# Three feature products of a step placed on two row halves of the TensorE array

## The chip, the cores and the metric

The kernel runs on one core of a Trainium2 chip. The time is that of the device for one execution of the whole program, in microseconds; where several executions were made, their median.

## What is computed

For each of 512 sequences, 128 steps follow one another. A step k takes 12 features of each sequence: four "flat" ones, of which the last (number 3) is replaced by the previous step's result from step 1 on, and eight "path" ones.

```python
def _tower(x, w_in, b_in, blocks):
    h = _leaky(x @ w_in + b_in)
    for w1, b1, w2, b2 in blocks:            # two blocks, 128x128 weights
        h = _leaky(_leaky(h @ w1 + b1) @ w2 + b2 + h)
    return h

def step(prev_delta, xk):
    fk, k = xk
    d = jnp.where(k == 0, fk[:, DELTA_IDX], prev_delta)
    fk = fk.at[:, DELTA_IDX].set(d)
    fe = _tower(fk[:, :N_FLAT], fw_in, fb_in, flat_blocks)
    pe = _tower(fk[:, N_FLAT:], pw_in, pb_in, path_blocks)
    h = _leaky(jnp.concatenate([fe, pe], axis=-1) @ cw1 + cb1)
    delta = jax.nn.sigmoid(h @ cw2 + cb2)[:, 0]
    return (delta, delta)
```

The output is delta for every step and sequence. Only the flat tower and the head depend on the step before; the path tower doesn't.

## The kernel before

Activations lie with the 128 hidden units on the partitions and the 512 sequences along the free axis. The flat tower and the head work in two groups of 256 columns (g = 0, 1), each with a PSUM bank of its own (`ps_flat`, `ps_head`), whose second half takes the feature product and the output product. The path tower works on all 512 columns at once (`ps_path1`, `ps_path2`), its hidden products in two halves of 256.

The hidden products (line 394), the head (L479 for the path's part, L484 for the flat part) and the output (L490) are fp32 and take two MATMUL instructions each, every one with a weight load (LDWEIGHTS). The feature products are different: `path_in` (L406) and `flat_x` (L450, once for each group) are fp32r, one MATMUL each. To keep the accuracy, features and weights are split into a high and a low part. The features' parts are written to memory in four chunks (`store_chunk`) and are loaded for each step in the order hi, hi, lo, lo into four 32-row quarters of a tile of 128 rows (`load_x`, L134); the weights `in_split` hold hi, lo, hi, lo of the weights in the same quarters. The rows that are not features are zero or, for the bias row, one. Each of the three feature products so runs over all 128 rows. `x_path` and `x_flat` are two tiles each, by the parity of the step.

The order of the work is written out by hand, once for each engine, in its `body(k, par)`. TensorE's (L493) is a software pipeline: body k holds the flat tower, head and output of step k, the last path products of step k + 1, the middle ones of k + 2, and the first ones of k + 3. `path_in(k + 3)` stands between the two halves of `path_2b(k + 1)`, with `combine_flat(k, 0)` behind it. `flat_x(k + 1, g = 0)` stands before `output(k, 0)` and `flat_x(k + 1, g = 1)` before `path_2a(k + 2)`.

Between the engines: ScalarE does the leaky activations of `p_in`, `p_mid`, `f_mid`, `f_res`, of the head (all L229) and the sigmoid `delta` (L277). VectorE adds bias and old value (`f_sum`, `p_sum`, L321), does the other leaky activations (L318), and `flat_delta` (L351): f_t = delta x its weight row + the product of flat_x, which needs the delta of its group and `s_f_x_mm` of its group. From f_t comes `f_in`, which the next step's `flat_1a` multiplies. SyncE issues the loads: `load_path` waits for path_in of two steps before, `load_flat` for both flat_x.

Of the kernel before, what the change touches and what calls it, by code (L numbers as in the profile page):

```python
# [9 lines left out]
GROUP_COLS = [(0, 256), (256, 512)]  # L10
GROUPS = len(GROUP_COLS)
HALF = BATCH // 2
QUAD = 32

CHUNK_STEPS = [8, 24, 48, 48]
CHUNKS = len(CHUNK_STEPS)
# [9 lines left out]
def build(nc, x, x_hi, x_lo, w, out):  # L26
# [4 lines left out]
    with ctx:  # L31
        def sb(name, shape, dt=fp32):
            return ctx.enter_context(nc.sbuf_tensor(name, shape, dt))
# [4 lines left out]
        def sem(name):  # L38
            return ctx.enter_context(nc.semaphore(name))
# [11 lines left out]
        cb2_col, cw2_rep = sb("cb2_col", [HID, 1]), sb("cw2_rep", [HID, HID])  # L51


        in_raw, in_split = sb("in_raw", [128, 2 * HID]), sb("in_split", [128, 2 * HID], fp32r)
        flat_in_w, path_in_w = in_split[:, 0:HID], in_split[:, HID:2 * HID]

        chunk_x = [sb(f"chunk_x{c}", [128, CHUNK_COLS[c]]) for c in range(CHUNKS)]
        chunk_hi = [sb(f"chunk_hi{c}", [128, CHUNK_COLS[c]], fp32r) for c in range(CHUNKS)]
        chunk_lo = [sb(f"chunk_lo{c}", [128, CHUNK_COLS[c]], fp32r) for c in range(CHUNKS)]

        x_flat = [sb(f"x_flat{p}", [128, BATCH], fp32r) for p in range(2)]
        x_path = [sb(f"x_path{p}", [128, BATCH], fp32r) for p in range(2)]

        p_in, p_mid1, p_mid2 = sb("p_in", [HID, BATCH]), sb("p_mid1", [HID, BATCH]), sb("p_mid2", [HID, BATCH])
        p_sum1, p_sum2 = sb("p_sum1", [HID, BATCH]), sb("p_sum2", [HID, BATCH])
# [18 lines left out]
        def second(b, g):  # L84
            lo, hi = GROUP_COLS[g]
            return b[g][:, hi - lo:2 * (hi - lo)]

        def cols(t, g):
            lo, hi = GROUP_COLS[g]
            return t[:, lo:hi]  # L90

        def half(t, h):
            return t[:, h * HALF:(h + 1) * HALF]

        s_in_zero, s_pads, s_in_loaded, s_in_hi, s_in_split = (
            sem(n) for n in ("s_in_zero", "s_pads", "s_in_loaded", "s_in_hi", "s_in_split"))
        s_w_loaded, s_columns, s_cw2, s_delta0 = (sem(n) for n in ("s_w_loaded", "s_columns", "s_cw2", "s_delta0"))
        s_chunk_loaded, s_chunk_hi, s_chunk_split, s_chunk_stored = (
            [sem(f"{n}{c}") for c in range(CHUNKS)]
# [31 lines left out]

        @block.sync
        def _(sp):
            def load_x(tile, loaded, rows, k, par):  # L134
                for q, part in enumerate((x_hi, x_hi, x_lo, x_lo)):
                    sp.dma_start(tile[par][q * QUAD + rows.start:q * QUAD + rows.stop, :].bitcast(fp32),
                                 part[k, rows, :]).then_inc(loaded[par], 16)

            def load_path(k, par):
                if not exists(k):  # L140
                    return
                if exists(k - 2):
                    sp.wait_ge(s_p_in_mm, k - 1)
                load_x(x_path, s_x_path, slice(N_FLAT, FEATS), k, par)

            def load_flat(k, par):
                if not exists(k):
                    return
                if exists(k - 2):
                    for g in range(GROUPS):  # L150
                        sp.wait_ge(s_f_x_mm[g], k - 1)
                load_x(x_flat, s_x_flat, slice(0, DELTA), k, par)

            def store_delta(k, par):
                if not exists(k):
                    return
                for g in range(GROUPS):
                    sp.wait_ge(s_delta[g], k + 1)
                sp.dma_start(out[k:k + 1, :], delta[par][0:1, :]).then_inc(s_stored[par], 16)

            def load_chunk(c):
                sp.dma_start(chunk_x[c][:, :], chunk_rows(x, c)).then_inc(s_chunk_loaded[c], 16)

            def store_chunk(c):
                sp.wait_ge(s_chunk_split[c], 1)
                sp.dma_start(chunk_rows(x_hi, c),
                             chunk_hi[c][:, :].bitcast(fp32)).then_inc(s_chunk_stored[c], 16)
                sp.dma_start(chunk_rows(x_lo, c),
                             chunk_lo[c][:, :].bitcast(fp32)).then_inc(s_chunk_stored[c], 16)

            def body(k, par):
                load_path(k, par)
                load_flat(k - 2, par)
                store_delta(k - 5, 1 - par)

            load_chunk(0)
            sp.wait_ge(s_in_zero, 1)
            for q in range(4):
                sp.dma_start(in_raw[q * QUAD:q * QUAD + FEATS + 1, :], w["inputs"]).then_inc(s_in_loaded, 16)
            sp.dma_start(hidden_w[:, :], w["hidden"]).then_inc(s_w_loaded, 16)  # L180
            sp.dma_start(delta[1][:, :], x[0, DELTA:DELTA + 1, :].to_broadcast([HID, BATCH])).then_inc(s_delta0, 16)
            store_chunk(0)
            sp.wait_ge(s_pads, 2)
            sp.wait_ge(s_chunk_stored[0], 32)
            body(0, 0)
            body(1, 1)
            for c in range(1, CHUNKS):
                load_chunk(c)
            for k in range(2, 6):
                body(k, k % 2)  # L190
            for c in range(1, CHUNKS):
                store_chunk(c)
            for c in range(CHUNKS):
                sp.wait_ge(s_chunk_stored[c], 32)
                for k in range(max(6, CHUNK_FIRST[c]), CHUNK_FIRST[c] + CHUNK_STEPS[c]):
                    body(k, k % 2)
            for k in range(STEPS, STEPS + 5):
                body(k, k % 2)
            for p in range(2):
                sp.wait_ge(s_stored[p], 8 * STEPS)  # L200

        @block.gpsimd
        def _(pool):
            pool.memset(in_raw[:, :], 0.0).then_inc(s_in_zero, 1)
            for tile in x_flat + x_path:
                last = pool.memset(tile[:, :].bitcast(fp32), 0.0)
            last.then_inc(s_pads, 1)
            pool.wait_ge(s_pads, 1)
            for tile in x_flat + x_path:
                last = pool.memset(tile[0:2 * QUAD, :].bitcast(fp32), 1.0)  # L210
            last.then_inc(s_pads, 1)
            pool.wait_ge(s_pads, 2)
            for c in range(1, CHUNKS):
                pool.wait_ge(s_chunk_loaded[c], 16)
                pool.tensor_copy(chunk_hi[c][:, :], chunk_x[c][:, :]).then_inc(s_chunk_hi[c], 1)
                pool.wait_ge(s_chunk_hi[c], 1)
                pool.tensor_tensor(chunk_lo[c][:, :], chunk_x[c][:, :], chunk_hi[c][:, :].bitcast(fp32),
                                   ALU.subtract).then_inc(s_chunk_split[c], 1)
# [80 lines left out]
        def _(dve):  # L299
# [3 lines left out]
            dve.tensor_tensor(chunk_lo[0][:, :], chunk_x[0][:, :], chunk_hi[0][:, :].bitcast(fp32),  # L303
                              ALU.subtract).then_inc(s_chunk_split[0], 1)

            dve.wait_ge(s_in_loaded, 64)
            dve.tensor_copy(in_split[:, :], in_raw[:, :]).then_inc(s_in_hi, 1)
            dve.wait_ge(s_in_hi, 1)
            for q in (1, 3):
                rows = slice(q * QUAD, (q + 1) * QUAD)  # L310
                dve.tensor_tensor(in_split[rows, :], in_raw[rows, :], in_split[rows, :].bitcast(fp32),
                                  ALU.subtract).then_inc(s_in_split, 1)

            dve.wait_ge(s_columns, 32)
            dve.tensor_copy(cw2_rep[:, :], column["cw2"].to_broadcast([HID, HID])).then_inc(s_cw2, 1)
# [76 lines left out]
        def _(pe):  # L392
# [7 lines left out]
            def path_in(k, par):  # L400
                if exists(k):
                    pe.wait_ge(s_x_path[par], filled(k, par))

                    if exists(k - 1):
                        pe.wait_ge(s_p1b_t, k)
                    pe.matmul(ps_path1[:, :], path_in_w, x_path[par][:, :], start=True, stop=True)\  # L406
                      .then_inc(s_p_in_mm, 1)

            def path_1a(k, h):
# [34 lines left out]
            def flat_x(k, par, g):  # L444
                if exists(k):
                    pe.wait_ge(s_x_flat[par], filled(k, par))

                    if exists(k - 1):
                        pe.wait_ge(s_f2b_t[g], k)
                    pe.matmul(second(ps_flat, g), flat_in_w, cols(x_flat[par], g), start=True, stop=True)\  # L450
                      .then_inc(s_f_x_mm[g], 1)

            def flat_1a(k, g):
# [39 lines left out]
            def body(k, par):  # L493
                flat_1a(k, 0)
                path_2a(k + 1, 1 - par, 1)
                flat_1a(k, 1)
                flat_1b(k, 0)
                combine_path(k, par, 0)
                flat_1b(k, 1)
                path_1b(k + 2, 0)  # L500
                flat_2a(k, 0)
                path_1b(k + 2, 1)
                flat_2a(k, 1)
                flat_2b(k, 0)
                combine_path(k, par, 1)
                flat_2b(k, 1)
                path_2b(k + 1, 0)
                path_in(k + 3, 1 - par)
                combine_flat(k, 0)
                path_2b(k + 1, 1)  # L510
                combine_flat(k, 1)
                flat_x(k + 1, 1 - par, 0)
                output(k, 0)
                path_1a(k + 3, 0)
                output(k, 1)
                path_1a(k + 3, 1)
                flat_x(k + 1, 1 - par, 1)
                path_2a(k + 2, par, 0)

            pe.wait_ge(s_w_loaded, 16)  # L520
            pe.wait_ge(s_in_split, 2)
            pe.wait_ge(s_cw2, 1)
            bodies(pe, body)

# [32 lines left out]
```

## Time and profile before

| | |
|---|---|
| Median of 3 runs | 1321.8 us (1321.71 to 1322.02) |
| The profiled execution's own time | 1322.16 us |
| Its span, first to last instruction | 1320.4 us |
| TensorE busy | 1296.7 us (98%), 6016 MATMULs |
| TensorE weight loads busy | 1071.2 us (81%), 6016 loads |
| VectorE busy | 853.9 us (65%) |
| ScalarE busy | 828.5 us (63%) |
| Mean granted TensorE clock | 0.999 of full speed |

The span leaves out 1.8 us of the execution's time, before the first and behind the last instruction. "Busy" of TensorE counts a matmul from its recorded start to a modelled end; matmuls are pipelined, so a new one begins before the record of the one before has ended. A MATMUL and its weight load are on two rows, PE and PEld. SPq is the queue of SyncE, from which DMAs are issued.

### The profile page before, as it was taken

Reading aid. Unit: us, or ns where it says so; the run is one execution under the profiler, and the core shown is the slowest. Engines: PE = TensorE matmul, PEld = TensorE weight load, DVE = VectorE, ACT = ScalarE, POOL = GpSimd, SP = SyncE. Lnnn points to the kernel's source line nnn. Section 1 sums busy time; section 2 is a strip of 40 time slices with the busy share of each in tenths; the row PEclk is TensorE's granted clock in tenths of the full one; section 3 lists DMA queues with packets and bytes.
Section 4 is the critical chain, followed back from the end, with each engine's and each line's share of the span. In section 5 each row is a group of like instructions: output and inputs, shape, how many; then the busy total and the mean of one; then the engine's idle time right before and its main releaser. Section 6 shows DMA issues by size and latency. Waiting matters only on the chain.

```text
span 1320.4 us, 18500 instructions
## 1 busy us (share of the span) xinstructions
PE 1296.7 (98%) x6016; PEld 1071.2 (81%) x6016; DVE 853.9 (65%) x1670; ACT 828.5 (63%) x1793; POOL 22.6 (2%) x19
## 2 busy tenths in 40 slices
PE   4999999999999999999999999999999999999998
PEld 2888888888888888888888888888888888888885
DVE  3666666666666666666666666666666666666665
ACT  2566666666666666666666666666666666666665
POOL 6000000000000000000000000000000000000000
PEclk9999999999999999999999999999999999999999
DMA  4400000000000000000000000000000000000000
GB/s 149 188 10 9 11 10 10 11 10 10 9 11 10 10 11 10 10 10 11 10 10 11 10 10 10 11 10 10 11 10 9 10 11 10 9 11 10 9 8 1
DMA packets 14022, 23.41 MB, mean 18 GB/s; under 512 B 6324, under 2 KB 6760, under 8 KB 13160
## 3 DMA queue, kind: packets, MB, share of 16 engines
q1 hardware_dynamic: 13640, 22.23, 5.7%
q8 instruction: 50, 0.82, 0.3%
q14 instruction: 44, 0.36, 0.1%
q10 hardware_dynamic: 288, 0.01, 0.0%
HBM read 15.66 MB, written 6.55 MB: 17 GB/s over the span
## 4 chain that ended last, share of the span: by engine, by line
PE 97%; DVE 1%; DMA 1%; ACT 0%; issue 0%; SPq 0%; ACTq 0%
PE ps_flat L394 34%; PE ps_path L394 34%; PE ps_head L479 8%; PE ps_head L484 8%; PE ps_head L490 8%; PE ps_path L406 2%; PE ps_flat L450 2%; DVE f_in L318 0%; DMA x_lo<-chunk_lo 0%; DVE f_t L351 0%; DMA chunk_x<-x 0%; DVE f_sum L321 0%; DVE p_sum L321 0%; DMA x_path<-x_lo 0%; ACT delta L277 0%
## 5 line engine op out<-in xcount | busy, mean ns | idle before, releaser
L229 ACT ACTIVATE f_mid<-ps_flat,columns_sb 128x256 f32<-128x256 f32 x512 | 242.4, 474 | 153.5 <-PE ps_flat L394 153.5
L394 PE MATMUL ps_path<-p_mid,hidden_w 128*128 128x256 f32 x1024 | 306.1, 381 | 0.8 <-ACT p_mid L229 0.8
L394 PE MATMUL ps_flat<-f_mid,hidden_w 128*128 128x256 f32 x1024 | 305.3, 380 | 0.0
L229 ACT ACTIVATE head<-ps_head,columns_sb 128x256 f32<-128x256 f32 x256 | 121.3, 474 | 246.0 <-PE ps_head L484 246.0
L394 PEld LDWEIGHTS ps_path<-p_mid,hidden_w 128*128 128x128 f32 x1024 | 195.9, 191 | 28.3 <-ACT p_mid L229 1.5
L394 PEld LDWEIGHTS ps_flat<-f_mid,hidden_w 128*128 128x128 f32 x1024 | 175.2, 189 | 46.2
L321 DVE SCALAR_TENSOR_TENSOR f_sum<-ps_flat,columns_sb,f_in 128x256 f32<-128x256 f32 x256 | 123.9, 484 | 129.1 <-PE ps_flat L394 129.1
L351 DVE SCALAR_TENSOR_TENSOR f_t<-delta,columns_sb,ps_flat 128x256 f32<-128x256 f32 x256 | 123.0, 480 | 98.3 <-ACT delta L277 93.3
L229 ACT ACTIVATE p_mid<-ps_path,columns_sb 128x512 f32<-128x512 f32 x256 | 174.8, 683 | 5.5 <-PE ps_path L394 5.5
L321 DVE SCALAR_TENSOR_TENSOR p_sum<-ps_path,columns_sb,p_in 128x512 f32<-128x512 f32 x128 | 96.1, 751 | 121.3 <-PE ps_path L394 121.3
L394 PE MATMUL ps_flat<-f_in,hidden_w 128*128 128x256 f32 x512 | 162.1, 398 | 5.1 <-DVE f_in L318 5.1
L394 PE MATMUL ps_path<-p_in,hidden_w 128*128 128x256 f32 x512 | 154.1, 384 | 1.6 <-ACT p_in L229 1.4
L394 PE MATMUL ps_flat<-f_res,hidden_w 128*128 128x256 f32 x512 | 153.0, 381 | 0.7 <-ACT f_res L229 0.7
L394 PE MATMUL ps_path<-p_res,hidden_w 128*128 128x256 f32 x512 | 153.1, 381 | 0.2 <-ACT p_res L229 0.2
L479 PE MATMUL ps_head<-p_res,hidden_w 128*128 128x256 f32 x512 | 152.8, 380 | 0.0
L490 PE MATMUL ps_head<-head,cw_rep 128*128 128x256 f32 x512 | 152.6, 380 | 0.2
L484 PE MATMUL ps_head<-f_res,hidden_w 128*128 128x256 f32 x512 | 152.4, 379 | 0.3 <-DVE f_res L318 0.3
L321 DVE SCALAR_TENSOR_TENSOR p_sum<-ps_path,columns_sb,p_res 128x512 f32<-128x512 f32 x128 | 96.1, 751 | 74.8 <-PE ps_path L394 74.8
L229 ACT ACTIVATE f_res<-f_sum 128x256 f32<-128x256 f32 x256 | 106.7, 417 | 58.5 <-DVE f_sum L321 58.4
L321 DVE SCALAR_TENSOR_TENSOR f_sum<-ps_flat,columns_sb,f_res 128x256 f32<-128x256 f32 x256 | 123.8, 484 | 17.5 <-PE ps_flat L394 3.3
L277 ACT ACTIVATE delta<-ps_head,cb_col 128x256 f32<-128x256 f32 x256 | 120.0, 469 | 10.0 <-PE ps_head L490 0.6
L450 PE MATMUL ps_flat<-x_flat,in_split 128*128 128x256 f32 x256 | 120.0, 469 | 0.0
(32 smaller groups left out, 1266.6 us busy)
## 6 DMA issues: line engine op xcount, KB each, us to landing
x_path<-x_hi SPq DMA_DIRECT2D x256, 16.0 KB
x_path<-x_lo SPq DMA_DIRECT2D x256, 16.0 KB
x_flat<-x_hi SPq DMA_DIRECT2D x256, 6.0 KB
x_flat<-x_lo SPq DMA_DIRECT2D x256, 6.0 KB
chunk_x<-x SPq DMA_DIRECT2D x2, 1152.0 KB, 7.8
x_hi<-chunk_hi SPq DMA_DIRECT2D x2, 1152.0 KB, 9.3
x_lo<-chunk_lo SPq DMA_DIRECT2D x2, 1152.0 KB, 10.8
out<-delta SPq DMA_DIRECT2D x128, 2.0 KB
```

The lines of the kernel that those rows point to most:

```text
L229: return act.activation(dst, src, ACT.Prelu, bias=bias, alpha=NEG)
L277: act.activation(cols(delta[par], g), second(ps_head, g), ACT.Sigmoid, bias=cb2_col[:, :]).then_inc(s_delta[g], 1)
L321: return dve.scalar_tensor_tensor(dst, products, bias, old, ALU.add, ALU.add)
L351: dve.scalar_tensor_tensor(f_t[g][:, :], cols(delta[1 - par], g), column["delta_w"], second(ps_flat, g), ALU.mult, ALU.add).then_inc(s_f_i ...
L394: return pe.matmul(dst, weight[w_name], src, start=True, stop=True)
L406: pe.matmul(ps_path1[:, :], path_in_w, x_path[par][:, :], start=True, stop=True)\
L450: pe.matmul(second(ps_flat, g), flat_in_w, cols(x_flat[par], g), start=True, stop=True)\
L479: pe.matmul(layer(ps_head, g), weight["cw1_path"], cols(p_res2[par], g), start=True, stop=False)
L484: pe.matmul(layer(ps_head, g), weight["cw1_flat"], f_res2[g][:, :], start=False, stop=True)\
L490: pe.matmul(second(ps_head, g), cw2_rep[:, :], head[g][:, :], start=True, stop=True)\
```

## The change

The two x tiles of a parity become one tile `x_both` of 128 rows: the path features (4 x 8 rows, the rest ones) in rows 0 to 63, the flat features (4 x 3 rows, the rest ones) in rows 64 to 127. The weights lie likewise in `in_split`, 128 columns wide instead of 256, packed without gaps between the four parts and with two bias rows (hi and lo). `path_in` now uses the array's rows 0 to 63 (`tile_position=(0, 0)`, 64 rows) and `flat_x` rows 64 to 127 (`tile_position=(64, 0)`, 64 rows). The sizes of the results and the columns streamed (512 and twice 256) stay as they were.

The three products now stand next to each other: `path_in(k + 3)` moves behind both halves of `path_2b(k + 1)`, both `flat_x(k + 1)` follow it, and `combine_flat(k, 1)` comes behind them.

[...] GpSimd fills two x tiles instead of four.

```diff
-        in_raw, in_split = sb("in_raw", [128, 2 * HID]), sb("in_split", [128, 2 * HID], fp32r)
-        flat_in_w, path_in_w = in_split[:, 0:HID], in_split[:, HID:2 * HID]
+        in_raw, in_lo, in_split = sb("in_raw", [128, HID]), sb("in_lo", [128, HID], fp32r), sb("in_split", [128, HID], fp32r)
+        path_in_w, flat_in_w = in_split[0:ROWS, :], in_split[ROWS:2 * ROWS, :]
...
-        x_flat = [sb(f"x_flat{p}", [128, BATCH], fp32r) for p in range(2)]
-        x_path = [sb(f"x_path{p}", [128, BATCH], fp32r) for p in range(2)]
+        x_both = [sb(f"x_both{p}", [128, BATCH], fp32r) for p in range(2)]
+        x_path = [t[0:ROWS, :] for t in x_both]
+        x_flat = [t[ROWS:2 * ROWS, :] for t in x_both]
...
-            def load_x(tile, loaded, rows, k, par):
+            def load_x(first, loaded, rows, k, par):
+                n = rows.stop - rows.start
                 for q, part in enumerate((x_hi, x_hi, x_lo, x_lo)):
-                    sp.dma_start(tile[par][q * QUAD + rows.start:q * QUAD + rows.stop, :].bitcast(fp32),
+                    sp.dma_start(x_both[par][first + q * n:first + (q + 1) * n, :].bitcast(fp32),
                                  part[k, rows, :]).then_inc(loaded[par], 16)
...
-            for q in range(4):
-                sp.dma_start(in_raw[q * QUAD:q * QUAD + FEATS + 1, :], w["inputs"]).then_inc(s_in_loaded, 16)
+            for first, rows, to in ((0, slice(N_FLAT, FEATS), HID), (ROWS, slice(0, DELTA), 0)):
+                n = rows.stop - rows.start
+                for q in range(4):
+                    sp.dma_start(in_raw[first + q * n:first + (q + 1) * n, :],
+                                 w["inputs"][rows, to:to + HID]).then_inc(s_in_loaded, 16)
+                for q in range(2):
+                    sp.dma_start(in_raw[first + 4 * n + q:first + 4 * n + q + 1, :],
+                                 w["inputs"][FEATS:FEATS + 1, to:to + HID]).then_inc(s_in_loaded, 16)
...
-            sp.wait_ge(s_pads, 2)
+            sp.wait_ge(s_in_lo, 1)
+            for first, n in ((0, N_PATH), (ROWS, DELTA)):
+                for row, rows in ((n, n), (3 * n, n), (4 * n + 1, 1)):
+                    block_of = slice(first + row, first + row + rows)
+                    sp.dma_start(in_split[block_of, :].bitcast(fp32),
+                                 in_lo[block_of, :].bitcast(fp32)).then_inc(s_in_split, 16)
+            sp.wait_ge(s_pads, 1)
             sp.wait_ge(s_chunk_stored[0], 32)
...
-            for q in (1, 3):
-                rows = slice(q * QUAD, (q + 1) * QUAD)
-                dve.tensor_tensor(in_split[rows, :], in_raw[rows, :], in_split[rows, :].bitcast(fp32),
-                                  ALU.subtract).then_inc(s_in_split, 1)
+            dve.tensor_tensor(in_lo[:, :], in_raw[:, :], in_split[:, :].bitcast(fp32), ALU.subtract).then_inc(s_in_lo, 1)
...
-                    pe.matmul(ps_path1[:, :], path_in_w, x_path[par][:, :], start=True, stop=True)\
+                    pe.matmul(ps_path1[:, :], path_in_w, x_path[par][:, :], start=True, stop=True, tile_position=(0, 0))\
                       .then_inc(s_p_in_mm, 1)
...
-                    pe.matmul(second(ps_flat, g), flat_in_w, cols(x_flat[par], g), start=True, stop=True)\
+                    pe.matmul(second(ps_flat, g), flat_in_w, cols(x_flat[par], g), start=True, stop=True,
+                              tile_position=(ROWS, 0))\
                       .then_inc(s_f_x_mm[g], 1)
...
                 path_2b(k + 1, 0)
-                path_in(k + 3, 1 - par)
                 combine_flat(k, 0)
                 path_2b(k + 1, 1)
+                path_in(k + 3, 1 - par)
+                flat_x(k + 1, 1 - par, 0)
+                flat_x(k + 1, 1 - par, 1)
                 combine_flat(k, 1)
-                flat_x(k + 1, 1 - par, 0)
                 output(k, 0)
                 path_1a(k + 3, 0)
                 output(k, 1)
                 path_1a(k + 3, 1)
-                flat_x(k + 1, 1 - par, 1)
                 path_2a(k + 2, par, 0)
```

TensorE's order in one step, before, from the first half of path_2b to flat_1a of group 1. The names behind the arrow's left are the PSUM banks, with their numbers; `p_mid2` is path_2b's operand, `p_in` path_1a's, `p_res1` path_2a's:

```order
L394 MATMUL ps_path2<-p_mid2,hidden_w 128x256
L406 MATMUL ps_path1<-x_path0,in_split 128x512
L484 MATMUL ps_head0<-f_res2_0,hidden_w 128x256
L484 MATMUL ps_head1<-f_res2_1,hidden_w 128x256
L450 MATMUL ps_flat0<-x_flat0,in_split 128x256
L490 MATMUL ps_head0<-head_0,cw2_rep 128x256
L394 MATMUL ps_path1<-p_in,hidden_w 128x256
L490 MATMUL ps_head1<-head_1,cw2_rep 128x256
L450 MATMUL ps_flat1<-x_flat0,in_split 128x256
L394 MATMUL ps_path2<-p_res1_1,hidden_w 128x256
L394 MATMUL ps_flat0<-f_in_0,hidden_w 128x256
L394 MATMUL ps_flat1<-f_in_1,hidden_w 128x256
```

Left out are the second halves of path_2b (behind the first L484), of path_1a (behind the second L490) and of path_2a (before the last row). The same stretch in the changed kernel, all rows but the second halves of path_1a and path_2a:

```order
L404 MATMUL ps_path2<-p_mid2,hidden_w 128x256
L495 MATMUL ps_head0<-f_res2_0,hidden_w 128x256
L404 MATMUL ps_path2<-p_mid2,hidden_w 128x256
L416 MATMUL ps_path1<-x_both0,in_split 128x512
L460 MATMUL ps_flat0<-x_both0,in_split 128x256
L460 MATMUL ps_flat1<-x_both0,in_split 128x256
L495 MATMUL ps_head1<-f_res2_1,hidden_w 128x256
L501 MATMUL ps_head0<-head_0,cw2_rep 128x256
L404 MATMUL ps_path1<-p_in,hidden_w 128x256
L501 MATMUL ps_head1<-head_1,cw2_rep 128x256
L404 MATMUL ps_path2<-p_res1_1,hidden_w 128x256
L404 MATMUL ps_flat1<-f_in_1,hidden_w 128x256
```

The three feature products have gone together between path_2b and combine_flat of group 1; the x_flat product of group 1 no longer stands between output and flat_1a.

SyncE's queue in the set-up, before and in the changed kernel, up to the first load of x:

```order
L162 DMA chunk_x0<-x 128x384
L179 DMA in_raw<-inputs 13x256 x4
L180 DMA hidden_w<-hidden 128x1280
L181 DMA delta1<-x 128x512
L166 DMA x_hi<-chunk_hi0 128x384
L168 DMA x_lo<-chunk_lo0 128x384
L136 DMA x_path0<-x_hi 8x512 x2
```

```order
L186 DMA in_raw<-inputs 8x128 x4
L189 DMA in_raw<-inputs 1x128 x2
L186 DMA in_raw<-inputs 3x128 x4
L191 DMA hidden_w<-hidden 128x1280
L192 DMA delta1<-x 128x512
L171 DMA x_hi<-chunk_hi0 128x384
L173 DMA x_lo<-chunk_lo0 128x384
L198 DMA in_split<-in_lo 8x128 x2
L198 DMA in_split<-in_lo 3x128 x2
L141 DMA x_both0<-x_hi 8x512 x2
```

Left out in the second are the first row, which is as before, and the repeated one-row copies of L189 and L198. Fourteen small DMAs have come ahead of the first load of x: eight before the stores of the first chunk, six behind them.

## Rows read from the trace of the kernel before

**Rows 1.** The page: busy time by engine, and the granted clock in 40 slices.

```profile
PE 1296.7 (98%) x6016; PEld 1071.2 (81%) x6016; DVE 853.9 (65%) x1670; ACT 828.5 (63%) x1793; POOL 22.6 (2%) x19
...
PEclk9999999999999999999999999999999999999999
```

**Rows 2.** The chain of waits in one middle step: start us, us, what.

```profile
602.74 0.43 PE ps_path L394 x2
603.17 0.23 PE ps_path L406
...
604.70 0.12 PE ps_flat L450
...
606.54 0.12 PE ps_flat L450
...
607.96 0.94 PE ps_flat L394 x4
...
612.78 0.43 PE ps_path L394 x2
```

**Rows 3.** Timeline around x_path: start us, us, engine, line, operation, operands.

```profile
602.44 0.43 DVE L318 SCALAR_TENSOR_TENSOR f_res<-f_sum 128x256 f32<-128x256 f32 x1
602.78 0.48 DVE L321 SCALAR_TENSOR_TENSOR f_sum<-ps_flat,columns_sb,f_res 128x256 f32<-128x256 f32 x1
602.80 0.19 PEld L406 LDWEIGHTS ps_path<-x_path,in_split 128*128 128x128 f32 x1
602.82 0.58 PE L406 MATMUL ps_path<-x_path,in_split 128*128 128x512 f32 x1
603.01 0.42 PEld L484 LDWEIGHTS ps_head<-f_res,hidden_w 128*128 128x128 f32 x2
```

**Rows 4.** Timeline of VectorE, ScalarE and TensorE around f_t of group 1.

```profile
606.18 0.47 ACT L277 ACTIVATE delta<-ps_head,cb_col 128x256 f32<-128x256 f32 x1
606.19 0.47 PE L450 MATMUL ps_flat<-x_flat,in_split 128*128 128x256 f32 x1
606.31 0.42 DVE L318 SCALAR_TENSOR_TENSOR f_in<-f_t 128x256 f32<-128x256 f32 x1
...
606.77 0.48 DVE L351 SCALAR_TENSOR_TENSOR f_t<-delta,columns_sb,ps_flat 128x256 f32<-128x256 f32 x1
...
607.28 0.42 DVE L318 SCALAR_TENSOR_TENSOR f_in<-f_t 128x256 f32<-128x256 f32 x1
...
607.63 0.69 DVE L318 SCALAR_TENSOR_TENSOR p_res<-p_sum 128x512 f32<-128x512 f32 x1
```

**Rows 5.** Weight loads of flat_1a, group 1, first and second half, from two windows.

```profile
607.76 0.19 PEld L394 LDWEIGHTS ps_flat<-f_in,hidden_w 128*128 128x128 f32 x1 [0.21 <-DVE f_in L318]
...
607.87 0.19 PEld L394 LDWEIGHTS ps_flat<-f_in,hidden_w 128*128 128x128 f32 x1
```

**Rows 6.** ScalarE's p_in in that step, and one fp32 product half.

```profile
604.25 0.59 ACT L229 ACTIVATE p_in<-ps_path 128x512 f32<-128x512 f32 x1
...
604.65 0.38 PE L490 MATMUL ps_head<-head,cw_rep 128*128 128x256 f32 x1
```

**Rows 7.** Set-up: SyncE's queue in the timeline, then the chain of waits.

```profile
1.22 1.62 SPq L179 DMA_DIRECT2D in_raw<-inputs  x4
...
3.28 0.44 SPq L181 DMA_DIRECT2D delta<-x  x1
4.31 0.33 SPq L166 DMA_DIRECT2D x_hi<-chunk_hi  x1
...
4.68 3.77 DMA x_lo<-chunk_lo
...
8.54 0.29 SPq L136
...
9.54 1.56 DMA x_path<-x_lo
...
11.23 0.78 PE ps_path L406
```

More of the change, by code:

```diff
@@ L12 @@
 HALF = BATCH // 2
-QUAD = 32
+ROWS = 64
+N_PATH = FEATS - N_FLAT
 CHUNK_STEPS = [8, 24, 48, 48]
@@ L93, in half @@
             return t[:, h * HALF:(h + 1) * HALF]
-        s_in_zero, s_pads, s_in_loaded, s_in_hi, s_in_split = (
-            sem(n) for n in ("s_in_zero", "s_pads", "s_in_loaded", "s_in_hi", "s_in_split"))
+        s_in_zero, s_pads, s_in_loaded, s_in_hi, s_in_lo, s_in_split = (
+            sem(n) for n in ("s_in_zero", "s_pads", "s_in_loaded", "s_in_hi", "s_in_lo", "s_in_split"))
         s_w_loaded, s_columns, s_cw2, s_delta0 = (sem(n) for n in ("s_w_loaded", "s_columns", "s_cw2", "s_delta0"))
@@ L143, in load_path @@
                     sp.wait_ge(s_p_in_mm, k - 1)
-                load_x(x_path, s_x_path, slice(N_FLAT, FEATS), k, par)
+                load_x(0, s_x_path, slice(N_FLAT, FEATS), k, par)
             def load_flat(k, par):
@@ L151, in load_flat @@
                         sp.wait_ge(s_f_x_mm[g], k - 1)
-                load_x(x_flat, s_x_flat, slice(0, DELTA), k, par)
+                load_x(ROWS, s_x_flat, slice(0, DELTA), k, par)
             def store_delta(k, par):
@@ L204, in _ @@
             pool.memset(in_raw[:, :], 0.0).then_inc(s_in_zero, 1)
-            for tile in x_flat + x_path:
-                last = pool.memset(tile[:, :].bitcast(fp32), 0.0)
+            for tile in x_both:
+                last = pool.memset(tile[:, :].bitcast(fp32), 1.0)
             last.then_inc(s_pads, 1)
             pool.wait_ge(s_pads, 1)
[L209 to L212, printed above, removed]
             for c in range(1, CHUNKS):
@@ L304, in _ @@
                               ALU.subtract).then_inc(s_chunk_split[0], 1)
-            dve.wait_ge(s_in_loaded, 64)
+            dve.wait_ge(s_in_loaded, 192)
             dve.tensor_copy(in_split[:, :], in_raw[:, :]).then_inc(s_in_hi, 1)
             dve.wait_ge(s_in_hi, 1)
-            for q in (1, 3):
-                rows = slice(q * QUAD, (q + 1) * QUAD)
-                dve.tensor_tensor(in_split[rows, :], in_raw[rows, :], in_split[rows, :].bitcast(fp32),
-                                  ALU.subtract).then_inc(s_in_split, 1)
+            dve.tensor_tensor(in_lo[:, :], in_raw[:, :], in_split[:, :].bitcast(fp32), ALU.subtract).then_inc(s_in_lo, 1)
             dve.wait_ge(s_columns, 32)
@@ L516, in body @@
                 path_1a(k + 3, 1)
-                flat_x(k + 1, 1 - par, 1)
                 path_2a(k + 2, par, 0)
             pe.wait_ge(s_w_loaded, 16)
-            pe.wait_ge(s_in_split, 2)
+            pe.wait_ge(s_in_split, 96)
             pe.wait_ge(s_cw2, 1)
```

## The prediction

> **What bounds the kernel now.** I read the page first. [...] A busy share alone says little for a pipelined engine, so I went to the chain of waits for one step in the middle. It consists of TensorE pieces only: from the path_2b piece at 602.74 to the next step's path_2b piece at 612.78 a step takes 10.04 us, and a hidden product (two instructions, at a pace of 0.22) takes 0.43. x_path takes 0.23 and each of the two x_flat products 0.12, so the three feature products cost 0.47 us of a step. One piece is longer than its work: the four halves from 607.96 take 0.94 where 0.87 would do [rows 2]. There flat_1a of group 1 waits 0.07.
>
> Next the timeline around x_path, with the weight loads. Each MATMUL has one of its own. The load of x_path runs from 602.80, under the product before it, and the load after it starts at 603.01. That is when x_path really begins to stream; its recorded start, 602.82, is too early. Its recorded end is 603.40, 0.39 after the real start [rows 3].
>
> The wait at flat_1a group 1 has a cause that this change touches. The chain is output g0, delta g0, f_t and f_in of group 0, then f_t and f_in of group 1. f_t of group 1 starts at 606.77. Its delta ended at 606.65 and f_in of group 0 at 606.73, and VectorE starts an operation up to 0.07 before the recorded end of the one before (p_res at 607.63, f_in ended at 607.70). What came last was x_flat g1, ended at 606.66 [rows 4]. Without it f_t could start at about 606.68, 0.09 earlier. f_in ends at 607.70, flat_1a's first weight load goes at 607.76 and its second at 607.87, which is when the product begins [rows 5]: an exposed weight load costs 0.11 us.
>
> **The change, part by part.** Sums are made against the profiled execution (1322.2 us, span 1320.4), 0.4 above the median of the three runs, 1321.8; what they add is put on the median. About 125 steps have all products. What a measurement of this kernel can't tell from no change is 0.2%, 2.6 us.
>
> *Leaving the old places* gives 0.23 + 0.12 + 0.12 = 0.47 us a step [rows 2].
>
> *x_flat g1 ahead of the delta chain.* The chain gets 0.09 shorter, but 0.12 of TensorE's work between output g0 and flat_1a g1 is gone too, so TensorE waits there 0.07 + 0.12 - 0.09 = 0.10: +0.03 a step.
>
> *combine_flat g0 directly after path_2b's first half.* It needs f_res of group 0, ended at 602.87 [rows 3]. With 0.06 to the weight load and 0.11 for it [rows 5] it starts at 603.04; the sequence has its place at 603.01 to 603.03. I take +0.01.
>
> [...]
>
> [...]
>
> *Set-up.* The in_raw copies on SP's queue go from 4 to 12, at 1.62 / 4 = 0.41 each: +3.2 us. SP now waits from 3.72 to 4.31 for the first chunk's split, which covers 0.6 of it, so the stores go out 2.7 later. Six small copies in_split<-in_lo, at 0.3 to 0.4 to issue, lie beside the 3.77 of the stores' flight. The first x_path load starts at 11.2 instead of 8.54, and the first product waits for it [rows 7]: +2.7 us. The fewer memsets are hidden.
>
> The sum is +16 + 2.7 = +19: **1341 us**.
>
> **The rivals.** *The tiles overlap and the change of division is free* (the other side, faster). [...] For it: weight loads already run under products [rows 3], and the halves share no rows and no bank. [...] Against it: nothing in this trace divides the array.
>
> [...]
>
> *The tiles don't overlap*, and the division is free: only the order is new. X = 0.47, a step 10.08, +5 + 2.7: 1330. For it: x_path streams alone now, and the next product starts when it is through [rows 3]. Against: nothing ties the two halves together.
>
> [...]
>
> **How the numbers follow.** The forecast (0.04 to 0.27 for each change of division) gets 0.50, its own range 1323 to 1375; free overlap 0.38; no overlap 0.12. The range 1300 to 1368 takes in the second and third and all but the dearest of the first. Faster by over 0.2% needs X under 0.39: free overlap, 0.38. Within 0.2% is X from 0.39 to 0.43, the cheapest changes: 0.07. Slower: 0.55. The sign hangs on a price of 0.04 us, so I am not sure of it.
>
> **What would show it.** In the changed kernel's chain of waits a step is 9.61 + X, with X from x_path's real start to that of combine_flat g1. *Right*: x_path's weight load starts only when path_2b's half has streamed, and combine_flat g1's only when x_flat g1 has, each leaving about 0.1; x_flat g0 starts within x_path; f_t of group 1 starts as soon as f_in of group 0 lets it; flat_1a g1 waits about 0.1; the first product starts at about 13.9. *Wrong*: both loads run under the product before (1313 or less), or x_flat g0 starts where x_path ends (1330), or p_in's later start shows as a wait of path_1a.

## The result and the profile after

The changed kernel takes **1350.2 us** (median of 4 runs, 1349.7 to 1350.9), the kernel before 1321.8 beside it. The ratio is 1.0216, with a 95% interval of 1.0198 to 1.0234: slower, by 28.5 us. The forecast was 1341, in a range of 1300 to 1368.

The page of the changed kernel, the lines that answer to [rows 1]:

```profile
PE 1323.4 (98%) x6016; PEld 1010.2 (75%) x6016; DVE 845.4 (63%) x1669; ACT 849.6 (63%) x1793; POOL 19.4 (1%) x13
...
PEclk9899999999999999999999999999999999999999
```

TensorE is as busy as before, 98%, though less is streamed one after another. That is the modelled busy time: a record also covers the wait that a weight load imposes (0.70 us for the two products at 608.77 below, 0.59 elsewhere). As a share of the span the page shows nothing of the loss. The chain of waits does, here for one middle step (start us, us, what), to be read beside [rows 2]:

```profile
603.22 0.43 PE ps_head L490 x2
...
608.41 0.32 PE ps_path L416
608.73 0.12 PE ps_flat L460
608.84 0.63 PE ps_head L495 x2
609.47 0.43 PE ps_head L501 x2
...
610.77 0.92 PE ps_path L404 x4
611.69 0.46 PE ps_flat L404 x2
...
612.57 0.88 PE ps_flat L404 x4
613.46 0.43 PE ps_head L490 x2
```

From 603.22 to 613.46 a step takes 10.24 us, 0.20 more than before. The feature group and combine_flat g1 behind it take 609.47 - 608.41 = 1.06, of which combine_flat's own work is 0.43: X = 0.63, where the three products took 0.47 when they stood apart. The three small excesses further down are waits (0.92 for 0.87, 0.46 and 0.88 for 0.43 and 0.87), 0.10 us together as the prediction had it, though in other places.

The timeline of TensorE and its weight loads around the group shows where 0.63 comes from (start us, us, engine, line, operation; the first row, from a window of its own, is path_2b's second half):

```profile
608.03 0.38 PE L404 MATMUL ps_path<-p_mid,hidden_w 128*128 128x256 f32 x1
...
608.34 0.18 PEld L416 LDWEIGHTS ps_path<-x_both,in_split 64*128 64x128 f32 x1 [0.33 <-issue]
608.34 0.50 PE L416 MATMUL ps_path<-x_both,in_split 64*128 64x512 f32 x1
608.34 0.29 PEld L460 LDWEIGHTS ps_flat<-x_both,in_split 64*128 64x128 f32 x2
608.34 0.50 PE L460 MATMUL ps_flat<-x_both,in_split 64*128 64x256 f32 x2
...
608.77 0.30 PEld L495 LDWEIGHTS ps_head<-f_res,hidden_w 128*128 128x128 f32 x2
608.77 0.70 PE L495 MATMUL ps_head<-f_res,hidden_w 128*128 128x256 f32 x2
```

The second half of path_2b starts at 608.03, so with the pace of 0.22 its place ends at 608.25. By the pattern of the kernel before, x_path's weight load would start at 608.03, under it ([rows 3]: 602.80). Here it starts at 608.34: 0.09 after the stream has ended. Then both halves of the array get their weights **at the same time** (608.34 and 608.34). By the same reading as for x_path in the kernel before, the real start of the two products is later than the recorded one; an estimate with the 0.11 of an exposed weight load [rows 5] puts it at about 608.45, when the load of the second flat product begins, and that product follows some 0.11 behind the first. With path's 512 columns beside them (0.23 by rounded figures [rows 2]) the last column is in at about 608.67. The next full-width weight load starts at 608.77, 0.10 later, not under the group, and takes its 0.11; the product starts at 608.88, where its second weight load stands. So: 0.09 + 0.11 to go in, 0.23 for the group, 0.10 + 0.11 to come out, 0.64 by these rounded figures.

**Behind the group** the chain that sets flat_1a g1 runs as described, with the x product gone from it (start us, us; VectorE and ScalarE in the same step):

```profile
609.94 0.47 ACT L290 ACTIVATE delta<-ps_head,cb_col 128x256 f32<-128x256 f32 x1
...
610.31 0.62 ACT L242 ACTIVATE p_res<-p_sum 128x512 f32<-128x512 f32 x1
...
610.83 0.47 ACT L290 ACTIVATE delta<-ps_head,cb_col 128x256 f32<-128x256 f32 x1
610.96 0.42 DVE L328 SCALAR_TENSOR_TENSOR f_in<-f_t 128x256 f32<-128x256 f32 x1
610.99 0.30 PEld L404 LDWEIGHTS ps_path<-p_res,hidden_w 128*128 128x128 f32 x2 [0.19 <-ACT p_res L242]
...
611.33 0.48 DVE L361 SCALAR_TENSOR_TENSOR f_t<-delta,columns_sb,ps_flat 128x256 f32<-128x256 f32 x1
```

f_t of group 1 starts at 611.33, 0.05 before the recorded end of f_in of group 0 (611.38) and 0.03 after its delta's (611.30); before, it started 0.04 after f_in's end [rows 4]. The first of the waits is new: path_2a's weight load waits for p_res, which ScalarE runs behind delta g0.

**The set-up.** SyncE's queue (start us, us), then the first product, to [rows 7]:

```profile
5.90 0.42 SPq L171 DMA_DIRECT2D x_hi<-chunk_hi  x1
6.37 0.43 SPq L173 DMA_DIRECT2D x_lo<-chunk_lo  x1
6.84 4.11 SPq L198 DMA_DIRECT2D in_split<-in_lo  x6
11.07 0.73 SPq L141 DMA_DIRECT2D x_both<-x_hi  x2
...
13.86 0.76 PE L416 MATMUL ps_path<-x_both,in_split 64*128 64x512 f32 x1 [13.86 <-DMA x_both<-x_lo]
```

The first product starts 2.6 us later than before, 13.86 instead of 11.23. A third item stood in no sum of the prediction. Early on flat_1a g1 waits for f_in, with TensorE idle for 3.3 us (4.1 in the kernel before), and then TensorE works on for a while at half of its full clock (0.50): a product of two instructions takes 0.85 us there instead of 0.43. Windows of the changed kernel (us from and to; length, busy time of PE, PEld, DVE, ACT, POOL; granted clock, DMA share, GB/s); the two left out, up to 42, are at 0.50 as well:

```profile
36.00:38.00 2.00, 1.81 (x4) 1.51 (x5) 0.74 (x2) 0.55 (x2) 0.00 (x0) 0.50 0.00 0
...
42.00:47.00 5.00, 5.00 (x24) 3.91 (x23) 3.24 (x6) 2.14 (x5) 0.00 (x0) 0.97 0.01 3
```

The same stretch in the kernel before:

```profile
34.00:36.00 2.00, 2.00 (x7) 1.65 (x8) 0.93 (x2) 1.26 (x3) 0.00 (x0) 0.67 0.00 0
36.00:38.00 2.00, 2.00 (x6) 1.57 (x5) 0.48 (x1) 0.63 (x2) 0.00 (x0) 0.50 0.00 0
38.00:40.00 2.00, 2.00 (x10) 1.65 (x9) 0.98 (x2) 0.95 (x2) 0.00 (x0) 0.98 0.00 0
```

As an estimate, the clock is taken to be either full or half, 0.50 being the lowest that any of these windows shows. With clock c a window of length t then holds 2t(1 - c) at half speed: 6.3 us after (from 36.0 on), 3.4 before, so 2.9 us more, which lose half of that, some 1.5 us. The account of this pair of executions: 124 steps x 0.197 (10.234 less 10.037, the medians of a step's length over the steady part) = 24.4, set-up 2.6, clock 1.5, together 28.5, where their spans differ by 28.7.

The clock's 1.5 us don't come from the change. The stretch at half speed is 3.4 us long in the profiles of *Both in the same half* and *The copies off SyncE's queue* below, which divide the array, and 6.8 us in that of *x_flat g1 earlier*, which doesn't (granted clock 0.61, 0.50, 0.50 and 0.68 in its windows of 2 us from 32 to 40). Two of the changed kernel's four executions have a mean granted clock of 0.999 and took 1349.7 and 1349.8 us, the other two 0.997 and 1350.7 and 1350.9. So the change itself costs about 1349.7 - 1321.8 = 27.9 us (the profiled execution of the kernel before has 0.999), of which step and set-up explain 27.0; 0.9 us stay unassigned, little more than the 0.7 by which the executions of the kernel before differ.

### The profile page after: what moved, and what is told of

It reads as the page before. It is cut to its first block, busy times and chain, and to the rows that moved or that the text cites. A ratio compares the mean times of both kernels' runs of the same rounds, so it can differ in the third digit from the quotient of the medians.

```text
span 1349.1 us, 18507 instructions
## 1 busy us (share of the span) xinstructions
PE 1323.4 (98%) x6016; PEld 1010.2 (75%) x6016; DVE 845.4 (63%) x1669; ACT 849.6 (63%) x1793; POOL 19.4 (1%) x13
## 4 chain that ended last, share of the span: by engine, by line
PE 98%; DVE 1%; SPq 1%; ACT 0%; issue 0%; DMA 0%; ACTq 0%
PE ps_path L404 34%; PE ps_flat L404 33%; PE ps_head L495 10%; PE ps_head L490 8%; PE ps_head L501 8%; PE ps_path L416 3%; PE ps_flat L460 1%; DVE f_in L328 0%; SPq L198 0%; SPq L186 0%; DVE f_sum L331 0%; DMA x_both<-x_lo 0%; DVE f_t L361 0%; DVE p_sum L331 0%; ACT p_in L242 0%
## 5 line engine op out<-in xcount | busy, mean ns | idle before, releaser
L404 PEld LDWEIGHTS ps_path<-p_mid,hidden_w 128*128 128x128 f32 x1024 | 196.6, 192 | 28.7 <-ACT p_mid L242 1.5
L404 PEld LDWEIGHTS ps_flat<-f_mid,hidden_w 128*128 128x128 f32 x1024 | 171.5, 189 | 50.4
L495 PE MATMUL ps_head<-f_res,hidden_w 128*128 128x256 f32 x512 | 166.7, 407 | 0.3 <-DVE f_res L328 0.3
L404 PE MATMUL ps_flat<-f_in,hidden_w 128*128 128x256 f32 x512 | 158.5, 391 | 4.2 <-DVE f_in L328 4.0
L404 PE MATMUL ps_path<-p_res,hidden_w 128*128 128x256 f32 x512 | 160.3, 395 | 0.3 <-ACT p_res L242 0.3
L490 PE MATMUL ps_head<-p_res,hidden_w 128*128 128x256 f32 x512 | 152.7, 380 | 0.0
L328 DVE SCALAR_TENSOR_TENSOR f_in<-f_t 128x256 f32<-128x256 f32 x256 | 113.0, 442 | 8.9
```

Of the source, the lines that this page charges most:

```text
L328: return dve.scalar_tensor_tensor(dst, src, NEG, src, ALU.mult, ALU.max)
L404: return pe.matmul(dst, weight[w_name], src, start=True, stop=True)
L490: pe.matmul(layer(ps_head, g), weight["cw1_path"], cols(p_res2[par], g), start=True, stop=False)
L495: pe.matmul(layer(ps_head, g), weight["cw1_flat"], f_res2[g][:, :], start=False, stop=True)\
```

## The experiments

*Theory A*: the price lies in each change between the full array and its halves, 0.20 us; the halves really run together. *Rival B*: the new order and its waits cost, not the tiles. *Rival C*: the overlap exists only in the records.

**The order alone.** The kernel before with the body of the changed one; every product over the full array.

```diff
+                combine_flat(k, 0)
                 path_2b(k + 1, 1)
+                path_in(k + 3, 1 - par)
+                flat_x(k + 1, 1 - par, 0)
+                flat_x(k + 1, 1 - par, 1)
```

> Full-array products as in the kernel before, in the changed kernel's order. Theory A (the price lies in going from the full array to halves and back): a step is 9.61 + 0.47 = 10.08 us, set-up unchanged, so 1321.8 + 5 = 1327 us, and no gap behind path_2b or ahead of combine_flat g1. Rival B (the new order's waits, p_in and p_res on ScalarE, are what costs): most of the loss remains, 1340 to 1348 us.

It took 1326.8 us, 1.003 of before (1.0018 to 1.0042). Its chain of waits around the group:

```profile
605.80 0.43 PE ps_path L394 x2
606.24 0.23 PE ps_path L406
606.47 0.24 PE ps_flat L450 x2
606.70 0.43 PE ps_head L484 x2
```

The group takes 0.47 with no gap before or behind it, though fp32r products stand between fp32 ones here too. The waits of 0.10 are all there, so the order costs about 4 us with them: 4.0 against the kernel before in executions made beside it (1322.8; the interval allows 2.4 to 5.6), 4.7 by the step's median (10.075 less 10.037, 124 times). Rival B falls: of the 28.5 us, some 24 come with the tiles. They split into 0.16 x 124 = 20 for X and 2.6 for the set-up that the tiles need; the rest, about 2 us, is hardly more than executions of one kernel differ by with the clock.

**The tiles alone.** The changed kernel with the old body, so that path_in and each flat_x stand alone between full-width products.

```diff
                 path_2b(k + 1, 0)
+                path_in(k + 3, 1 - par)
                 combine_flat(k, 0)
                 path_2b(k + 1, 1)
-                path_in(k + 3, 1 - par)
-                flat_x(k + 1, 1 - par, 0)
-                flat_x(k + 1, 1 - par, 1)
                 combine_flat(k, 1)
+                flat_x(k + 1, 1 - par, 0)
                 output(k, 0)
...
                 path_1a(k + 3, 1)
+                flat_x(k + 1, 1 - par, 1)
```

> Half-array products in the order of the kernel before, so three separate places a step, each with a change of division in and out. Theory A: in the changed kernel's trace each change costs 0.20 us (0.09 to 0.10 of tail and an exposed weight load of 0.11), 0.40 for each place; a step is 10.04 + 3 x 0.40 less the wait of 0.07 that this covers = 11.17 us, and the time 1322 + 141 + 3 of set-up = 1466 us. Rival B: the old order brings the old time back, 1322 + 3 = 1325 us.

It took 1463.2 us, 1.1059 of before (1.1044 to 1.1074). The suspected cost, tripled, gives a step of 11.14 us against 11.17 expected. Its chain, at two of the three places:

```profile
601.94 0.43 PE ps_path L416
602.37 0.63 PE ps_head L495 x2
...
603.86 0.31 PE ps_flat L460
604.17 0.63 PE ps_head L501 x2
```

x_path takes 0.43 instead of 0.23, x_flat 0.31 instead of 0.12, and the product behind each 0.63 instead of 0.43. The price is the same whether 512 or 256 columns stand between: 0.19 to 0.20 in and 0.20 out. Rival B, with 1325, falls here as well.

**Both in the same half.** Flat features and weights get tiles of their own and also lie in rows 0 to 63.

```diff
-                              tile_position=(ROWS, 0))\
+                              tile_position=(0, 0))\
```

> The changed kernel with the flat products in rows 0 to 63 as well, in x and weight tiles of their own. Theory A with real overlap of the two halves: without it the group takes 0.47 instead of 0.23, the changes of division stay, a step is 10.23 + 0.24 = 10.47 us, 1350 + 30 = 1380 us. Rival C (the overlap in the records is only how starts are recorded, and the group streams one after another anyway): as the changed kernel, 1350 us.

It took 1379.5 us, 1.0427 of before (1.0412 to 1.0441). The chain:

```profile
599.71 0.43 PE ps_path L423
600.13 0.23 PE ps_flat L467 x2
600.37 0.63 PE ps_head L501 x2
```

Here the flat products come one after another behind x_path: X = 0.43 + 0.23 + 0.63 - 0.43 = 0.86, which is 0.47 + 0.39. The overlap of the changed kernel is real and worth 0.23 to 0.24 us a step, 29 us in all. Rival C falls.

**One half alone.** path_in in rows 0 to 63 at its old place; flat_x runs over all 128 rows, with zero weights in rows 0 to 63.

```diff
-        path_in_w, flat_in_w = in_split[0:ROWS, :], in_split[ROWS:2 * ROWS, :]
+        path_in_w, flat_in_w = in_split[0][0:ROWS, :], in_split[1][:, :]
...
-                    pe.matmul(second(ps_flat, g), flat_in_w, cols(x_flat[par], g), start=True, stop=True,
-                              tile_position=(ROWS, 0))\
+                    pe.matmul(second(ps_flat, g), flat_in_w, cols(x_flat[par], g), start=True, stop=True)\
```

> The order of the kernel before; path_in in rows 0 to 63 as in the changed kernel, flat_x over all 128 rows with a full-height weight tile. One place a step with a change in and out. Theory A: 0.195 in and 0.197 out, as at that place in e2_tiles, so a step is 10.04 + 0.39 = 10.43 us, 1322 + 49 + 3 of set-up = 1374 us. Rival: the price comes only where a half stands beside the other half, 1325 us.

It took 1374.9 us, 1.0392 of before (1.0374 to 1.0409). Its chain, at x_path and at one flat_x:

```profile
608.69 0.43 PE ps_path L423
609.12 0.63 PE ps_head L501 x2
...
610.61 0.12 PE ps_flat L467
610.73 0.43 PE ps_head L507 x2
```

A pair of changes costs its 0.39 to 0.40 (the step's median is 10.43, 10.04 before) with no second half beside it, and flat_x, whole again, pays nothing.

**Fewer rows, undivided array.** The kernel before with 112 rows in the feature products instead of 128.

```diff
-                    pe.matmul(ps_path1[:, :], path_in_w, x_path[par][:, :], start=True, stop=True)\
+                    pe.matmul(ps_path1[:, :], path_in_w[0:112, :], x_path[par][0:112, :], start=True, stop=True)\
```

> The kernel before with the feature products over rows 0 to 111 instead of 0 to 127 (the rows left out are zeros), no array position given. [...] Rival: any number of rows other than that of its neighbours is paid for, three places a step, about 1465 us.

If only a division of the array is paid for, the time is that of the kernel before, 1322 us. It took 1323.6 us; the ratio of 1.0011 (1.0002 to 1.0021) stands against 1.11 for the rival. In its chain of waits the products take the old 0.23 and 0.12:

```profile
603.86 0.23 PE ps_path L406
...
605.39 0.12 PE ps_flat L450
```

So a row count other than the neighbours' isn't by itself what is paid for. The 1.2 us that it took more are the step's median, which grew by 0.009; why it grew wasn't tried. Nor was a product of 64 rows without a position given, or any other division than into row halves, so what exactly marks a product as one of a divided array stays open.

**The copies off SyncE's queue.** The changed kernel; the set-up's six copies go to ScalarE's queue.

```diff
-            sp.wait_ge(s_in_lo, 1)
+            act.wait_ge(s_in_lo, 1)
...
-                    sp.dma_start(in_split[block_of, :].bitcast(fp32),
+                    act.dma_start(in_split[block_of, :].bitcast(fp32),
```

> The changed kernel with the six copies in_split<-in_lo issued from ScalarE's queue. In the changed kernel they hold SyncE's queue from 6.84 to 10.95, and the first load of x waits behind them. Theory: off that queue the stores' flight ends last (x_lo issued at 6.37 to 6.80, in flight 3.8), the first load goes at 10.3 and the first product at about 13.1 instead of 13.86: 0.8 us less, 1349.4 us. Rival: the copies or the stores land no sooner, and the time stays 1350.2 us.

It took 1350.5 us, and the theory fell. The chain of waits of this run:

```profile
6.34 4.63 DMA x_lo<-chunk_lo
...
11.05 0.29 SPq L141
...
14.03 0.78 PE ps_path L416
```

The store of the chunk's low part flies 4.63 us, and SyncE, which waits for it, issues the first load of x at 11.05, where the changed kernel did at 11.07. The expectation had taken the 3.8 from the kernel before; in the changed kernel the store flies 4.6 us too (issued at 6.37), so it lands at 10.97, as the last copy leaves the queue (10.95). Copies and store end together there; taking one off gains nothing. Why the store takes longer than in the kernel before, where no small copies are under way beside it, wasn't tried.

**x_flat g1 earlier, in the kernel before.** The part of the prediction that spoke of a gain, by itself.

```diff
                 output(k, 1)
+                flat_x(k + 1, 1 - par, 1)
                 path_1a(k + 3, 1)
-                flat_x(k + 1, 1 - par, 1)
```

> The kernel before, with x_flat of group 1 ahead of the second half of path_1a instead of behind it. If f_t of group 1 waited for it, the chain from output g0 to flat_1a g1 is up to 0.09 us shorter with TensorE's work unchanged, so the wait of 0.07 at flat_1a g1 goes: a step 9.97 us, 1321.8 - 9 = 1313 us. Rival: f_t of group 1 waits for its delta or for f_in of group 0 anyway and the wait stays, 1322 us.

It took **1314.7 us**, 0.9934 of before (0.9921 to 0.9946), 8 us less than the kernel before beside it (1322.8), and beats both kernels. Its chain:

```profile
603.96 0.12 PE ps_flat L450
...
605.81 0.86 PE ps_flat L394 x4
```

VectorE in the same step, f_in of group 0 and f_t of group 1:

```profile
604.16 0.42 DVE L318 SCALAR_TENSOR_TENSOR f_in<-f_t 128x256 f32<-128x256 f32 x1
604.53 0.48 DVE L351 SCALAR_TENSOR_TENSOR f_t<-delta,columns_sb,ps_flat 128x256 f32<-128x256 f32 x1
```

f_t of group 1 now starts 0.05 before f_in's recorded end, where it started 0.04 behind it [rows 4]. The last four halves take 0.86 instead of 0.94 [rows 2]; the wait is gone, and a step is 9.97 us, which is TensorE's own work: 22 products of 0.432 and 0.47 for the features. By the same sum one feature group a step on the tiles can't come near it: 9.50 + 0.63 = 10.13 even if no product waited.

## Why the prediction was right, and where its terms were off

- *A step is 9.61 + X* held: with X = 0.63 it gives 10.24, measured 10.234. So did its parts: the order alone gave 10.08 (median 10.075, expected 10.08), and x_flat g1 moved away from the delta chain frees f_t.
- *X = 0.34 + 2 x 0.11 = 0.56* was mis-sized in both terms, with opposite signs. No run shows the 0.34 of this sum, which took the weight loads of the two halves to come in turn: in the timeline both start at 608.34, and the group takes 0.23 (0.47 less the 0.24 that *Both in the same half* shows for the overlap). The change of division is dearer: 0.20 each instead of 0.11, since the exposed weight load of 0.11 comes with a tail of 0.09 to 0.10, which I had left out. It lies between my 0.11 and my upper bound of 0.27. The price alone would have added 0.17 to 0.18 us a step to the forecast; the group took 0.11 of it back. So it is partly luck that 1341 came near: the 0.07 that is left makes some 8 of the 9 us between it and 1350.
- *The way in and out.* In the timeline the full array's weights aren't loaded under a divided product, nor the other way: the loads start at 608.34 and 608.77, 0.09 and 0.10 after the stream before them has ended. With the 0.11 of the exposed load that makes 0.20 us in and 0.20 out.
- *The chances.* I gave slower 0.55, and said that the sign hangs on a price of 0.04 us. So the direction was held for hardly more likely than not, though the way to it was the one forecast. The forecast's own range, 1323 to 1375, doesn't follow from its 0.04 to 0.27: with 0.27 each way X is 0.34 + 0.54 = 0.88, a step 10.49 and the time 1381.
- *Free overlap* (0.38) was wrong in its second half only. Both halves start at 608.34, and without their overlap the time is 29 us longer (*Both in the same half*); but the way in and out costs 0.20 each. Its 1313 came from the 0.34 with no price added, and the range's 1300 from X = 0.23, x_path's time alone.
- *Waits of 0.10* came out as 0.10, but I had put all of it at flat_1a g1. It is 0.06 at path_2a (p_res behind delta g0 on ScalarE, a queue that I hadn't followed), 0.02 at flat_1a g0 and 0.02 at flat_1a g1.
- *Set-up +2.7*, measured +2.6, but by another way: the stores went out 1.6 us later, not 2.7, since an in_raw copy took 0.3 to issue and not 0.41; the copies of in_split took 0.68 each, not 0.3 to 0.4, and held the queue until 10.95.
- *Missing*: 0.9 us that no term explains, and the half-speed clock at the start, some 1.5 us that come and go between executions of either kernel.

## What to carry to other kernels

The products on the two row halves ran beside each other for real, but each passage between the full array and a half cost a tail and an exposed weight load, 0.20 us. So count the passages beside the columns saved: one pair a step cost 0.40 to save 0.24. Before dividing the array, look whether the small product stands on a dependence chain; here moving one 0.12 us product by one place was worth 8 us, by removing a wait that the busy share of 98% didn't show.

## What the runs showed of the hardware beyond that

The price of a passage was the same within 0.01 us at all places tried, all of them between fp32 products over the full array and fp32r products in 64 rows: for 256 and 512 columns, alone, with the other half beside it, or with a second product in the same half behind it (a pair costs 0.39 to 0.40 in each).

At the start GpSimd's subtraction and VectorE's f_in meet. In the changed kernel (start us, us):

```profile
30.70 5.16 POOL L230 TENSOR_TENSOR chunk_lo<-chunk_x,chunk_hi 128x2304 fp32r<-128x2304 f32 x1
...
31.38 4.76 DVE L328 SCALAR_TENSOR_TENSOR f_in<-f_t 128x256 f32<-128x256 f32 x1
```

f_in, 0.42 us in the steady part, takes 4.76 and ends at 36.14, 0.28 after GpSimd's instruction. What holds f_in for that long isn't shown. TensorE stood idle for 3.3 us over it, and when it went on the granted clock was 0.50 of full speed, up to 42 us. No run here took the meeting away: in each an f_in takes 4.7 to 5.3 us at this place.
